# Second FFN of a two-layer block: gate and up weights held in the array, the second product placed between their blocks, three result buffers stored tile by tile

## What is computed

```python
router_logits = jnp.einsum('sbh,eh->sbe', hidden_states, router_w)
routing_indices = jnp.argmax(router_logits, axis=-1)
for e in range(E):
    mask = (routing_indices == e)[..., None]
    xe = jnp.where(mask, hidden_states, 0.0)
    g = jnp.einsum('sbh,ih->sbi', xe, gate_w[e])
    u = jnp.einsum('sbh,ih->sbi', xe, up_w[e])
    ye = jnp.einsum('sbi,hi->sbh', jax.nn.silu(g) * u, down_w[e])
    out = out + jnp.where(mask, ye, 0.0)
...
x = x + jnp.tanh(g_ffn[1]) * _L1_ffn_ref(_layernorm(x, axis=-1), ...)
```

## Time and profile before

| | us |
|---|---|
| median of 3 runs | 825.15 |
| lowest, highest | 824.63, 825.51 |
| the profiled execution | 822.23 |
| its span, from the first instruction to the last event | 820.5 |
| first matmul of `second_ffn`'s products | at 716.2 |

### The profile page before, as it was taken

The page is one execution under the profiler, slowest core; times in us unless marked ns, Lnnn a source line. Parts: engine busy times, 40 slices in busy tenths (PEclk is TensorE's granted clock), DMA queues, the critical chain, the costliest instruction groups (busy, mean ns, idle before and its releaser), DMA issues. The chain is left out here.

```text
span 820.5 us, 30377 instructions
## 1 busy us (share of the span) xinstructions
PE 771.0 (94%) x10574; PEld 632.3 (77%) x10579; DVE 616.2 (75%) x2394; ACT 548.7 (67%) x1109; POOL 469.1 (57%) x876
## 2 busy tenths in 40 slices
PE   4999999998999989999999999999999998888895
PEld 2777777776788868888888888888888886367774
DVE  5899999998777767888888887878888787434442
ACT  2687888786555568777777777777777774155652
POOL 6555777772011265767667767667767674224444
PEclk9999999999999999999999999999999999999998
DMA  8805999500200000000000000000000000122000
GB/s 230 293 2 173 276 258 242 128 1 3 71 1 0 0 2 2 3 7 7 7 7 0 7 7 7 7 7 0 7 7 7 7 7 5 41 73 63 25 29 18
DMA packets 56160, 41.69 MB, mean 51 GB/s; under 512 B 3897, under 2 KB 51651, under 8 KB 55856
## 3 DMA queue, kind: packets, MB, share of 16 engines
q1 hardware_dynamic: 52400, 36.39, 16.8%
q0 software_dynamic: 2272, 4.27, 1.6%
q10 hardware_dynamic: 1440, 0.40, 0.3%
HBM read 18.07 MB, written 23.44 MB: 51 GB/s over the span
## 5 line engine op out<-in xcount | busy, mean ns | idle before, releaser
L1678 PE MATMUL l_pv<-l_Z,l_probs 128*128 128x129 f32 x1024 | 164.4, 284 | 3.0 <-ACT l_probs L1506 1.4
L1678 PEld LDWEIGHTS l_pv<-l_Z,l_probs 128*128 128x128 f32 x1024 | 138.3, 191 | 21.8 <-issue 5.2
L1439 POOL TENSOR_TENSOR l_qk_lo<-w,l_qk_hi 128x512 f16<-128x512 f32 x128 | 144.5, 1159 | 0.6 <-ACT l_qk_hi L1500 0.4
L1161 DVE SCALAR_TENSOR_TENSOR x_sb<-l_pv,l_inv,x_sb 128x128 f32 (+1 forms) x256 | 89.8, 351 | 33.7 <-DVE l_inv L1148 6.5
L1496 ACT ACTIVATE w<-l_qk_bank 128x512 f32<-128x512 f32 x124 | 74.1, 597 | 53.3 <-PE l_qk_bank L52 51.6
L52 PE MATMUL l_tz<-M,cT 128*128 128x512 f16 x384 | 104.1, 380 | 0.5 <-ACT l_Z L1511 0.3
L1506 ACT ACTIVATE l_probs<-l_b 128x512 f32<-128x512 f32 x128 | 72.7, 594 | 44.4 <-PE l_b L1644 44.2
L520 DVE TENSOR_REDUCE n_shared<-fold_bank 128x4 f32<-128x512 f32 x128 | 87.4, 684 | 9.5 <-PE fold_bank L735 9.3
L1138 DVE TENSOR_REDUCE l_neg_max<-l_a 128x4 f32<-128x512 f32 x128 | 83.2, 681 | 2.2 <-PE l_a L1622 2.1
L1500 ACT ACTIVATE l_qk_hi<-w 128x512 f16<-128x512 f32 x124 | 77.4, 624 | 1.1
L1511 ACT ACTIVATE l_Z<-l_tz 128x512 f32<-128x512 f32 x124 | 74.1, 597 | 4.9 <-PE l_tz L52 1.4
(11 more groups left out here) (291 smaller groups left out, 2287.6 us busy)
## 6 DMA issues: line engine op xcount, KB each, us to landing
expert_rows<-empty_row SPq DMA_DIRECT2D x8, 2178.0 KB, 23.6
x_sb<-expert_rows SPq DMA_DIRECT2D x36, 66.0 KB, 2.4
x_sb<-in_x SPq DMA_DIRECT2D x4, 512.0 KB, 6.5
ctx_sb<-in_ctx SPq DMA_DIRECT2D x4, 512.0 KB, 7.7
w<-in_L_ffn_w SPq DMA_DIRECT2D x1, 2048.0 KB, 9.2
w_raw<-in_L_ffn_gate_w SPq DMA_DIRECT2D x1, 1408.0 KB, 9.9
w_raw<-in_L_ffn_up_w SPq DMA_DIRECT2D x1, 1408.0 KB, 12.0
downT<-in_L_ffn_down_w SPq DMA_DIRECT2D x2, 512.0 KB, 4.0
```

Of the source, the lines that this page charges most:

```text
L1161: nc.vector.scalar_tensor_tensor(out=total, in0=O[:, h, 0:P], scalar=inv[:, j:j + 1], in1=total, op0=ALU.mult, op1=ALU.add).then_inc(summe ...
L1439: nc.gpsimd.tensor_tensor(qk_lo[:, w, m, Q * u:Q * u + Q].rearrange("p t n -> p (t n)"), qk[:, u, m, :], qk_hi[:, w, m, Q * u:Q * u + Q].r ...
L1678: last = nc.tensor.matmul(pv_bank[m % 2][:, h * (P + 1):(h + 1) * (P + 1)], probs[:, 2 * m + h, :], Z[:, w, 2 * m + h, :], start=True, sto ...
```

## The change

Gate and up trade operands: blocks of 128, 128 and 96 columns of the expert's weights are loaded into the array and the tile's 128 tokens stream past, so the products come out already transposed (hidden width on the partitions, tokens along the row), in `first_product`, three matmuls for each of six blocks. `transpose_hidden`, `hT_bank` and ACT's copy to `hidT` are gone; `silu` and `hid` grow from 352 to 384 columns, and DVE clears a corner of four banks instead of two. `hid` itself is the operand of the second product, whose three matmuls are put between the blocks: gate 0, second 0, gate 1, second 1, up 0, gate 2, second 2, up 1, up 2. The second product has two banks, chosen by the parity of the tile, and TensorE's waits stand at the head of a tile's work: for `hid` of the tile two before, and for the result of the tile four before. Results have three buffers of three tiles, and POOL waits for each tile's result before its store. In the first step 4 keep-awake matmuls replace 8.

```diff
--- before.py
+++ after.py
@@ -1771,6 +1771,7 @@
     STEPS = TILES // U
+    RESULTS = 3
...
@@ -1784,21 +1785,19 @@
-        silu = sb("silu", [P, 2, I1])
-        hid = sb("hid", [P, 2, I1])
-        hidT = sb("hidT", [P, 2, WIDE])
-        result = sb("result", [P, 2, U, P])
+        silu = sb("silu", [P, 2, WIDE])
+        hid = sb("hid", [P, 2, WIDE])
+        result = sb("result", [P, RESULTS, U, P])
         taker = sb("taker", [P, 2])
-        token = sb("token", [P, 2, U], mybir.dt.uint32)
-        t_bank, out_bank, *bank = [ctx.enter_context(nc.psum_tensor(f"f1_bank{n}", [P, 512], F32)) for n in range(8)]
-        gate_bank, up_bank, hT_bank = bank[0:2], bank[2:4], bank[4:6]
-        first_bank = (t_bank, *hT_bank)
+        token = sb("token", [P, RESULTS, U], mybir.dt.uint32)
+        t_bank, side_bank, *bank = [ctx.enter_context(nc.psum_tensor(f"f1_bank{n}", [P, 512], F32)) for n in range(8)]
+        gate_bank, up_bank, out_bank = bank[0:2], bank[2:4], bank[4:6]
+        first_bank = (t_bank, side_bank, out_bank[1])
...
@@ -1821,7 +1820,7 @@
             def _(dve):
-                for t in hT_bank:
+                for t in (*gate_bank, *up_bank):
...
@@ -1834,15 +1833,16 @@
                     dve.wait_ge(silu_ready, U * i + v + 1)
-                    nc.vector.tensor_tensor(hid[:, w, :], up_bank[w][:, 0:I1], silu[:, w, :], ALU.mult).then_inc(hid_ready, 1)
-                def results(i, v, half_i, p):
+                    nc.vector.tensor_tensor(hid[:, w, :], up_bank[w][:, 0:WIDE], silu[:, w, :], ALU.mult).then_inc(hid_ready, 1)
+                def results(i, v, w):
+                    p = i % RESULTS
                     if v == 0:
-                        if not isinstance(half_i, int) or half_i:
-                            dve.wait_ge(stored[p], 16 * U * half_i)
+                        if i >= RESULTS:
+                            dve.wait_ge(stored[p], 16 * U * (i // RESULTS))
...
                     dve.wait_ge(down_done, U * i + v + 1)
-                    nc.vector.scalar_tensor_tensor(out=result[:, p, v, :], in0=out_bank[:, 0:P], scalar=k.tg[:, 3:4],
+                    nc.vector.scalar_tensor_tensor(out=result[:, p, v, :], in0=out_bank[w][:, 0:P], scalar=k.tg[:, 3:4],
...
@@ -1854,9 +1854,9 @@
                         if v < 2 and live(-1):
-                            results(i - 1, v + 1, half_i - 1 + p, 1 - p)
+                            results(i - 1, v + 1, (p + v) % 2)
                         if v == 2 and live(0):
-                            results(i, 0, half_i, p)
+                            results(i, 0, (p + v) % 2)
...
@@ -1867,13 +1867,12 @@
-                def scatter(i, p):
-                    last = isinstance(i, int) and i == STEPS - 1
+                def scatter(i):
+                    p = i % RESULTS
...
                     for v in range(U):
-                        if v == 0 or last:
-                            pool.wait_ge(result_ready, U * i + (v + 1 if last else U))
+                        pool.wait_ge(result_ready, U * i + v + 1)
...
@@ -1882,11 +1881,11 @@
                     if live(-1):
-                        scatter(i - 1, 1 - p)
+                        scatter(i - 1)
...
                 every_step(pool, step)
-                for p in range(2):
-                    pool.wait_ge(stored[p], 16 * U * ((STEPS + 1 - p) // 2))
+                for p in range(RESULTS):
+                    pool.wait_ge(stored[p], 16 * U * len(range(p, STEPS, RESULTS)))
...
@@ -1911,19 +1910,13 @@
                     act.wait_ge(gate_done, U * i + v + 1)
-                    nc.scalar.activation(silu[:, w, :], gate_bank[w][:, 0:I1], ACT.Silu).then_inc(silu_ready, 1)
-                def hidden_transposed(n, w):
-                    act.wait_ge(hidT_moved, n + 1)
-                    nc.scalar.activation(hidT[:, w, :], hT_bank[w][:, 0:WIDE], ACT.Copy).then_inc(hidT_ready, 1)
+                    nc.scalar.activation(silu[:, w, :], gate_bank[w][:, 0:WIDE], ACT.Silu).then_inc(silu_ready, 1)
...
                             gated(i, v, (p + v) % 2)
-                        if live(0) and not (begins and v == 0) or live(-1) and v == 0:
-                            hidden_transposed(U * i + v - 1, (p + v + 1) % 2)
...
@@ -1960,59 +1953,67 @@
-                def first_products(i, v, p, e, need):
-                    if need:
+                def first_product(n, v, p, w, e, m, c):
+                    T = [t[:, p, v * P:v * P + P] for t in (T_hi, T_lo)]
+                    hi, lo, bank, done = ((k.gate_hi, k.gate_lo, gate_bank, gate_done), (k.up_hi, k.up_lo, up_bank, up_done))[m]
+                    c0, height = CHUNKS[c]
+                    weights = [t[:, bass.ds(e, 1), c0:c0 + height].rearrange("p a n -> p (a n)") for t in (hi, lo)]
+                    last = both_products(nc, bank[w][0:height, c * P:c * P + P],
+                                         [(weights[0], T[0]), (weights[1], T[0]), (weights[0], T[1])])
+                    if c == len(CHUNKS) - 1:
+                        last.then_inc(done, 1)
+                def second_product(n, w, e, c):
+                    height = CHUNKS[c][1]
+                    last = nc.tensor.matmul(out_bank[w][:, 0:P], hid[0:height, w, c * P:c * P + P],
+                                            k.downT[0:height, c, bass.ds(e, 1), :].rearrange("p a n -> p (a n)"),
+                                            start=c == 0, stop=c == len(CHUNKS) - 1, skip_group_check=True)
+                    if c == len(CHUNKS) - 1:
+                        last.then_inc(down_done, 1)
+                def products(n, i, v, p, e, need, behind):
+                    w = n % 2
+                    if behind is not None:
+                        pe.wait_ge(hid_ready, n - 1)
+                        if n > 3:
+                            pe.wait_ge(result_ready, n - 3)
+                    if e is not None and need:
                         pe.wait_ge(T_lo_ready, U * i + need)
-                    T = [t[:, p, v * P:v * P + P] for t in (T_hi, T_lo)]
-                    w = (p + v) % 2
-                    for hi, lo, bank, done in ((k.gate_hi, k.gate_lo, gate_bank, gate_done), (k.up_hi, k.up_lo, up_bank, up_done)):
-                        weights = [t[:, bass.ds(e, 1), :].rearrange("p a n -> p (a n)") for t in (hi, lo)]
-                        both_products(nc, bank[w][:, 0:I1], [(T[0], weights[0]), (T[0], weights[1]), (T[1], weights[0])]).then_inc(done, 1)
-                def transpose_hidden(n, w):
-                    pe.wait_ge(hid_ready, n + 1)
-                    for c, (c0, height) in enumerate(CHUNKS):
-                        last = nc.tensor.transpose(hT_bank[w][0:height, c * P:c * P + P], hid[:, w, c0:c0 + height], k.ident[:, :])
-                    last.then_inc(hidT_moved, 1)
-                def second_product(n, w, e):
-                    pe.wait_ge(hidT_ready, n + 1)
-                    if not isinstance(n, int) or n:
-                        pe.wait_ge(result_ready, n)
-                    for c, (_, height) in enumerate(CHUNKS):
-                        last = nc.tensor.matmul(out_bank[:, 0:P], hidT[0:height, w, c * P:c * P + P],
-                                                k.downT[0:height, c, bass.ds(e, 1), :].rearrange("p a n -> p (a n)"),
-                                                start=c == 0, stop=c == len(CHUNKS) - 1)
-                    last.then_inc(down_done, 1)
+                    for c in range(len(CHUNKS)):
+                        if e is not None:
+                            first_product(n, v, p, w, e, 0, c)
+                        if behind is not None:
+                            second_product(n - 2, w, behind, c)
+                        if e is not None and c:
+                            first_product(n, v, p, w, e, 1, c - 1)
+                    if e is not None:
+                        first_product(n, v, p, w, e, 1, len(CHUNKS) - 1)
...
                         n = U * i + v
-                        if live(0):
-                            first_products(i, v, p, now[v], v + 1 if begins else U if v == 0 else 0)
+                        if v < 2:
+                            behind = was[v + 1] if live(-1) else None
+                        else:
+                            behind = now[0] if live(0) else None
+                        if v == 2 and not live(0):
+                            continue
+                        products(n, i, v, p, now[v] if live(0) else None, v + 1 if begins else U if v == 0 else 0, behind)
                         if begins and v == 1:
-                            keep_awake(nc, k, out_bank, 8)
-                        if live(0) and not (begins and v == 0) or live(-1) and v == 0:
-                            transpose_hidden(n - 1, (p + v + 1) % 2)
-                        if v == 0 and live(1) and not begins:
+                            keep_awake(nc, k, side_bank, 4)
+                        if v == (2 if begins else 0) and live(1):
```

(34 more changed lines are left out.)

## The result

| | before | after |
|---|---|---|
| median of the runs | 824.32 us (823.04 to 825.51) | 827.35 us (827.03 to 830.24) |
| profiled execution | 822.23 us, span 820.5 | 830.24 us, span 828.5 |
| first product of the stage to the last store | 716.21 to 814.73, 98.5 us | 718.12 to 822.70, 104.6 us |
| granted clock over the span | 0.997 | 0.984 |

The ratio is 1.0042, with a 95% interval of 1.0026 to 1.0058: the changed kernel is 3.0 us slower. The forecast was 828.6. That is not all of it, though. The kernel before takes some 10 us less on two other chips (8 and 9). The changed kernel is 18.9 us slower than it on chip 8, and on chip 9 it is 15.2 us slower in the form with its second product put ahead (experiments 2 and 3).

What follows compares the result with a forecast made beforehand. It took TensorE's sequencer as the changed kernel's bound, 7.55 us a step against 7.26: register operations 5.4 and 1.0, opening 0.7, waits 0.45. That gave +3.5 us, 825.15 + 3.5 = 828.6; range 814 to 835, its own case 824.5 to 834.

Steps and rivals of the forecast that it cites:

- Register operations: TensorE's sequencer: 27 fused and 18 low at 0.12 us, ten shifts and masks at 0.10; with load and waits 7.55 a step.
- the opening: Head of each step on TensorE's sequencer: loading the experts' word, 0.7 us until the first shift.
- Array work: TensorE's matmuls: a tile's 18 short products 1.00 us, second product 0.67, next rows' transposes 0.33; 5.34 us a step.
- The rival that the array is the bound: Constant block offsets fold into instructions, leaving six operations a tile; steps of 5.8 us, 808.0 us in all; chance 0.10.
- a bank wait of 0.46: TensorE stalls for DVE's result once a step, 0.46 us, if the tile between takes 1.67 us; none at 2.2 or more.
- the prediction's own 2.14 us: From a tile's last up matmul through DVE's `hid`, `T_lo` and `result` to TensorE's restart: 2.14 us.
- Form of the gaps: TensorE's blocks in a tile: starts 0.24 us apart, with an idle gap "issue" in each, as sign of being right.
- No wait for `result`: Sign of being right: with two banks TensorE does not wait for DVE's `result` in steps of 7.5 us.
- Stores 1.29 apart behind a drain of 4.5 us: POOL's last stores 1.29 us apart; the last begins 4.55 us after the last up product, at 818.2.
- The clock: Rival: TensorE falls to 1.2 instead of 2.4 GHz, array needs 10.7 us a step, some +43, 868 us; chance 0.04.
- The sum: Whole stage: second step from 724.2, eleven steps of 7.55, last 6.4, store 4.55 later; +3.5 us on the span, 828.6.
- the old offset of 2.9: Median of the runs taken to stand 2.9 us above the profiled execution, as before: 825.15 + 3.5 = 828.6.

Runs made afterwards that it cites:

- experiments 2 and 3: Chip 8: changed kernel rerun unaltered, 830.63 us against 811.72 for the kernel before; chip 9: changed kernel with second product whole ahead of its blocks, 828.27 against 813.04.
- the experts fixed: Expert numbers set when the program is written, no register operations or word load, chip 2: changed kernel so altered 807.06 us, kernel before so altered 813.42 us.
- the one kept without check: Changed kernel taking the last step's expert numbers from registers and loading the experts' word without its bounds check: 821.31 us, ratio 0.9969 to the kernel before.
- the experts kept: Changed kernel taking the last step's expert numbers from registers, about four plain register operations a step fewer: 824.17 us, ratio 1.0009 to the kernel before, chip 2.

## Why the prediction was right, and what it didn't see

*Register operations.* Count right (234 fused, 311 = 234 + 77 plain). Price right: tile 0 has fourteen on line 52 between 757.2 and 759.4, and five of line 1968 among them, 0.12 each; 0.10 a plain one by experiment. Predicted 7.55 a step, measured 7.70; the sequencer was the bound, with a slope near one. The 0.15 isn't at the opening (0.75 from the load of the word to the first shift, a wait among it, against 0.7 + 0.11 in the sum). By the starts in the trace, over the six steps from 748.7 us on, the 45 address operations take 5.7 us a step instead of 5.4: a fused one 0.124 and the plain one behind it 0.113, but a few 0.15 to 0.28. Shifts and masks take 1.0 as forecast, opening and waits 0.99 instead of 1.15.

*Array work.* Mis-sized, with no effect. A part of the second product between blocks takes 0.28 and not the 0.22 it takes in a row, so a tile is 1.83 instead of 1.67 and a step 3 x 1.83 + 0.33 = 5.8 instead of 5.34; measured 5.84 with the experts fixed. The rival that the array is the bound gave 5.8 with a bank wait of 0.46, the right number for another reason: the steps of 5.84 have no such wait, and by the prediction's own 2.14 us it should still be 0.3 with a tile of 1.83. That term was too large and cost nothing only because the sequencer hid it.

*Form of the gaps.* Wrong. I expected blocks 0.24 apart with a gap in each. Starts in the changed kernel (timeline of PE: start us, length us, engine, line, what):

```profile
758.30 0.22 PE L52 MATMUL f_bank<-f_T_hi,w_hi 128*128 128x128 f16 x1
758.36 0.22 PE L52 MATMUL f_bank<-f_T_hi,w_lo 128*128 128x128 f16 x1
758.41 0.22 PE L52 MATMUL f_bank<-f_T_lo,w_hi 128*128 128x128 f16 x1
758.47 0.44 PE L1968 MATMUL f_bank<-downT,f_hid 128*128 x2
758.74 0.22 PE L52 MATMUL f_bank<-f_T_hi,w_hi 128*128 128x128 f16 x1
```

Two blocks and a part take the array 2 x 0.17 + 0.28 = 0.62 us and the sequencer 2 x 0.24 + 0.12 = 0.60. Inside a tile they keep pace; the sequencer's surplus, the opening and the shifts, shows at the heads. In the step shown it is 0.77 us ahead of tile 0 and 0.53, 0.24 and 0.30 in the first block and part of the three tiles, 1.84 in all, about what lies between 5.84 and 7.64.

*No wait for `result`.* Right. *Stores 1.29 apart behind a drain of 4.5 us:* right, 818.2 for the last up product, then (timeline of POOL):

```profile
821.41 0.98 POOL L1879 DMA_INDIRECT out<-f_result,f_token  x1 [0.30 <-DVE f_result L1845]
822.70 0.98 POOL L1879 DMA_INDIRECT out<-f_result,f_token  x1 [0.31 <-issue]
```

*The clock.* Right for the steady steps, 1.00. In the second step it did fall, behind a wait of 1.7 us for `T_lo`:

```profile
724.00:728.00 4.00, 2.24 (x22) 1.76 (x20) 1.44 (x4) 1.79 (x5) 1.20 (x2) 0.92 0.35 82
728.00:732.00 4.00, 4.00 (x36) 3.84 (x35) 0.81 (x2) 0.98 (x2) 0.99 (x1) 0.65 0.34 79
```

Matmuls of 128 columns start 0.105 apart there, half speed, 1.2 GHz. The wait alone doesn't do it: with the product ahead TensorE is as idle from 724 to 728 us (2.31 of 4.00 busy against 2.24), and its clock stays at 1.00. The price is small: the fourteen loads of the word span 101.2 us here and 100.6 in that kernel.

*The sum.* The profiled stage is 6.1 us longer, not 3.5: eleven steps 0.15 too long are 1.65, the clock up to 0.6, the first step 0.15 (the second step's first product starts 8.14 us into the stage instead of 8.0). The medians say 3.0. The profiled execution lies 2.9 above its median and that of before 2.1 below; adding the old offset of 2.9 was no better than adding none, and the errors cancel. So 828.6 against 827.35 is closer than the working earned.

*What it didn't see.* The sum takes 7.26 us a step as the kernel's own, and notes in passing that DVE starts 1.2 us late and that "the rows don't say why". That was the term to doubt. On chip 8 the step of before is 6.2, the difference in steps is 1.5 instead of 0.45 us, and the change costs 18.9 us. The time itself, 830.63, is still near the forecast, because the sequencer's bound is the same on every chip; the forecast difference of 3.5 us is not, and that it came out at 3.0 is luck of the chip on which both kernels were first run. Had I set the new bound against what the old kernel needs (6.03 of array) beside what it took, the case would have shown.

What makes the late start stays open. Known is: it occurs in the first profile of the kernel before; on chip 2 in the kernel before with the experts fixed (three steps of 7.0), in the changed kernel with the experts fixed and in the one kept without check; in no profile of chips 8 and 9, not in the changed kernel's own two, and not on chip 2 with the experts kept or with two banks and stores by tile. In the four profiles that have them none lies before the stage's first store. In the first profile `result` starts 0.8 to 0.9 us after the end of the step's third store in eight steps, and within 0.05 in the other two; from 753 to 783 us `T_hi` starts 0.6 us after the end of the second store, as long as it takes after free transposes. That is as if TensorE's work, or the word of its end, stood still while POOL issues a store. But on chip 8 the same stores at the same places delay nothing, so stores alone don't do it. The records put the product's end 1.2 us before its reader starts. By the Trainium skill (Perfetto Trace Analysis, Tensor Engine Instruction) a record of TensorE starts with its prefetch and its end is computed, not observed, so TensorE may have been held up inside records that look whole. That `result`, ACT's copy of `T_hi` and the next `silu` all start late fits that; no run proves it. Whether a stall for the bank brings on the next one, and whether stores one by one instead of three in a row end it, wasn't tried alone on a chip that shows it.

## What to carry to other kernels

Count the register operations of an engine's sequencer before cutting its work into shorter instructions whose addresses depend on a register: each costs its start-to-start time (0.10 to 0.12 us here), not its recorded 36 or 46 ns, and the bound shows in no busy share. When a step takes longer than the work you can add up, explain the difference before you compare with it; what isn't explained may be gone on the next chip. And the cheap part of a change can be the good one: the second bank and the stores by tile, without the new order of the products, together took 14 us off on chip 2, and each alone 1 to 3 where the kernel before was already fast.

## What was unexpected in the hardware

- The same kernel takes 821 to 824 us in three sets of runs (two of them on chip 2) and 812 to 813 on chips 8 and 9. The profiles put it into one stage (98.5 us against 87.9) at the same granted clock, 0.997.
- In that stage the readers of TensorE's results start 0.5 to 1.3 us late in some profiles, and only in steps in which POOL issues stores, and in others not at all, with the stores at the same places. Why is open.
- A part of the second product, two passes of full precision, takes 0.28 us between half-precision blocks and 0.22 in a row.
- The load of one word into a register with its check holds TensorE's sequencer for 0.75 us; leaving the bounds check out gives back 0.26.
